# GNN kernel on one core: GpSimd makes histogram digits, ScalarE zeroes the sums, SyncE reads the rows of two steps at a time

## The reference

```python
# layer 0: attention over edges, two heads of 64
rel_t_enc = jnp.cos((last_update[src] - t)[:, None] * time_w + time_b)
edge_attr = jnp.concatenate([rel_t_enc, msg], axis=-1)
q, k, v = x @ Wq + bq, x @ Wk + bk, x @ Wv + bv
e = edge_attr @ We
alpha = sum(q[dst] * (k[src] + e)) / 8        # per head
a = segment_softmax(alpha, dst)
out = segment_sum((v[src] + e) * a, dst) + x @ Wskip + bskip
x = layernorm(x + out)
# layer 1: the same edges the other way round: gathered at dst, summed at src
agg = segment_sum(edge_weight[:, None] * x[dst], src)
x = layernorm(x + agg @ W.T + b)
```

## Time and profile before

| | |
|---|---|
| median of 3 runs | 9757.03 us (9748.06 to 9765.64) |
| the profiled execution | 9753.79 us, its span 9752.1 us |
| busy: DVE, PE, POOL, ACT | 88%, 78%, 68%, 52% |
| setup | 0 to 342 us |
| layer 0 and its norm | 342 to 5240 us |
| layer 1, with pairs | 5240 to 9347 us |
| the last steps of segments | 9347 to 9653 us |

### The profile page before, as it was taken

One profiled execution on the slowest core, in us unless ns is written; L12 is line 12 of the kernel. 1 busy time (PEld: TensorE's weight loads), 2 busy tenths in 40 slices (PEclk: granted clock), 3 DMA queues, 4 the chain that ended last, 5 costly groups with the idle time before them and its releaser, 6 DMA issues. The chain is left out here.

```text
span 9752.1 us, 272152 instructions
## 1 busy us (share of the span) xinstructions
PE 7647.0 (78%) x52868; PEld 7179.5 (74%) x52869; DVE 8623.8 (88%) x21301; ACT 5102.7 (52%) x20838; POOL 6585.4 (68%) x6871
## 2 busy tenths in 40 slices
PE   6477777777777777777765777888888888888865
PEld 2477777777777777777765777788888888888854
DVE  5899999999999999999988666799999999999968
ACT  2277777777777777777762333333333333333300
POOL 0477777777777777777754777777777777777720
PEclk8689889888988888888885555587888887878888
DMA  6477767667666777766652222355555555556554
GB/s 193 109 180 179 177 177 180 177 176 180 178 178 177 179 177 178 179 179 177 178 126 64 74 74 74 99 152 150 152 152 152 152 152 150 153 150 153 152 138 116
DMA packets 1631706, 1484.67 MB, mean 152 GB/s; under 512 B 792007, under 2 KB 1363043, under 8 KB 1631203
## 3 DMA queue, kind: packets, MB, share of 16 engines
q1 hardware_dynamic: 1374244, 848.34, 35.8%
q0 software_dynamic: 257088, 632.95, 23.1%
HBM read 1225.51 MB, written 254.87 MB: 152 GB/s over the span
## 5 line engine op out<-in xcount | busy, mean ns | idle before, releaser
L817 POOL DMA_INDIRECT kv<-kv_scratch,arena x3136 | 3250.7, 1037 | 1238.1 <-issue 839.8
L869 POOL DMA_INDIRECT message_scratch<-ohT,idx x3232 | 3100.3, 959 | 1086.1 <-issue 956.5
L1261 ACT ACTIVATE ohT<-bank,kv 128x128 f32<-128x128 f32 x3232 | 923.9, 369 | 2609.2 <-PE bank L1063 1866.5
L1154 ACT ACTIVATE arena<-arena,weights 128x65 f32<-128x65 f32 x7040 | 1771.7, 337 | 2.4 <-PE bank L982 2.3
L1077 PE MATMUL bank<-oh,kve 128*128 128x128 f32 x8640 | 1377.4, 319 | 140.9 <-DVE arena L1838 107.9
L1063 PE MATMUL bank<-acc,oh 128*128 x6464 | 1284.9, 361 | 214.4 <-ACT ohT L1262 213.6
L982 PE MATMUL bank<-arena,oh 128*128 128x130 f32 x7040 | 1162.1, 317 | 288.0 <-DVE acc L1670 282.3
L1077 PEld LDWEIGHTS bank<-oh,kve 128*128 128x128 f32 x8640 | 1230.3, 224 | 163.8 <-issue 151.7
L1063 PEld LDWEIGHTS bank<-acc,oh 128*128 128x128 f32 x6464 | 1142.8, 265 | 259.1 <-issue 258.3
L982 PEld LDWEIGHTS bank<-arena,oh 128*128 128x128 f32 x7040 | 1045.5, 226 | 369.9 <-issue 300.3
L973 PE MATMUL bank<-arena,ohT 128*128 128x128 f32 x7040 | 1093.4, 307 | 0.0
(11 more groups left out here) (232 smaller groups left out, 12885.1 us busy)
## 6 DMA issues: line engine op xcount, KB each, us to landing
kve<-message_scratch SPq DMA_DIRECT2D x2160, 129.0 KB
kve<-nodes_scratch SPq DMA_DIRECT2D x880, 256.0 KB
feat<-in_edge_attr_dram SPq DMA_DIRECT2D x880, 96.0 KB
feat<-block_scratch SPq DMA_DIRECT2D x812, 98.0 KB
arena<-q_scratch SPq DMA_DIRECT2D x880, 64.0 KB
message_scratch<-ohT,idx POOLq DMA_INDIRECT x3232
kv<-kv_scratch,arena POOLq DMA_INDIRECT x3136
feat<-in_edge_attr_dram SPq DMA_DIRECT2D x880, 32.0 KB
```

The lines of the kernel that those rows point to most:

```text
L817: pool.indirect_dma_start(kv[:, k, g, :], None, kv_d, bass.IndirectOffsetOnAxis(ap=group_rows[:, half, k * G + g, 0:1].bitcast(I32), axis= ...
L869: pool.indirect_dma_start(msg_d, bass.IndirectOffsetOnAxis(ap=idx[:, k, g:g + 1], axis=0), sum_ring[:, k % RING1, g, :], None).then_inc(s_ ...
L1154: op = act.activation(wv[:, st.k % 2, g, h, :], vR[:, st.k, g, h, :], ACT.Copy, scale=weights[:, st.k // ROUND, g, st.k % ROUND, h:h + 1])
L1261: act.activation(sum_ring[:, st.k % RING1, g, 0:C], banks[2 + st.k % 2][:, g * P:(g + 1) * P], ACT.Copy, scale=taken[:, st.k, g, 2:3])
```

## The change

1. POOL makes the digits `h_lo` and `h_hi` at the start, from the moment that DVE is done with `raw` (`s_hist` 3), with a scratch `h_ten` for the product that one fused DVE operation did before. It also writes the high one-hots, seven comparisons of 128x128 a chunk in place of one DVE operation. DVE keeps the low one-hots, PE waits for both.
2. ACT zeroes `acc` by a copy of a broadcast zero, after the last reader of the histogram (`s_hist` 25). DVE's memset is gone; its first addition to `acc` waits for ACT.
3. In the last steps (`pairs` False) SP reads the six row numbers of two steps at once, and DVE makes the differences between the first and the second addition instead of after the third.

```diff
+            def whole(out, at):
+                pool.wait_ge(s_hist, at)
+                pool.tensor_scalar(out, out, MAGIC, None, ALU.add).then_inc(s_hist, 1)
+                pool.wait_ge(s_hist, at + 1)
+                pool.tensor_scalar(out, out, MAGIC, None, ALU.subtract).then_inc(s_hist, 1)
+
+            pool.wait_ge(s_hist, 3)
+            pool.wait_ge(s_tw, NT + 1)
+            pool.wait_ge(s_const, 3)
+            pool.tensor_scalar(h_lo, srcf_t[:, 0:THIST], 1.0 / P, -(P - 1) / (2.0 * P), ALU.mult, ALU.add).then_inc(s_hist, 1)
+            whole(h_lo, 4)
+            pool.wait_ge(s_zero, 16 * (4 + -(-NT // PIECE)))
+            pool.wait_ge(s_hist, 6)
+            pool.tensor_scalar(h_hi, h_lo, 1.0 / 16, -7.5 / 16, ALU.mult, ALU.add).then_inc(s_hist, 1)
+            whole(h_hi, 7)
+            pool.wait_ge(s_hist, 9)
+            pool.tensor_scalar(h_ten, h_hi, -16.0, None, ALU.mult).then_inc(s_hten, 1)
+            pool.wait_ge(s_hten, 1)
+            pool.tensor_tensor(h_lo, h_lo, h_ten, ALU.add).then_inc(s_hist, 1)
+            pool.wait_ge(s_ndump, 16 * NDUMPS)
+            for j in range(H_CHUNKS):
+                n = min(P, THIST - j * P)
+                wait(pool, s_hmm, j - 1)
...
+                for b in range(7):
+                    op = pool.tensor_scalar(h_oh[j % 2][1][:, 0:n, b], h_hi[:, j * P:j * P + n], float(b), None, ALU.is_equal)
+                op.then_inc(s_hohi, 1)
...
                     pe.wait_ge(s_hoh, j + 1)
+                    pe.wait_ge(s_hohi, j + 1)
...
+            act.wait_ge(s_tab, 2)
+            act.wait_ge(s_hist, 25)
+            act.activation(acc[:, :], zero[:, 0:1].to_broadcast([P, NB * HEADS * HB]), ACT.Copy).then_inc(s_acc0, 1)
...
-            dve.tensor_scalar(h_lo, srcf_t[:, 0:THIST], 1.0 / P, -(P - 1) / (2.0 * P), ALU.mult, ALU.add).then_inc(s_hist, 1)
-            halves(h_lo, P, 4)
...
-                dve.tensor_tensor(h_oh[j % 2][1][:, 0:n, :], h_hi[:, j * P:j * P + n].unsqueeze(2).to_broadcast([P, n, 7]),
-                                  irow[:, 0:7].unsqueeze(1).to_broadcast([P, n, 7]), ALU.is_equal).then_inc(s_hoh, 1)
...
-            dve.memset(acc[:, :], 0.0)
...
+                if isinstance(st.s, int) and st.s == 0:
+                    dve.wait_ge(s_acc0, 1)
...
-                rows = several(mybir.EngineType.SP, seg_row_i[0:1, bass.ds(q, SEGMENT)], TRASH // 2 - P)
+                if k % at_once == 0:
+                    found = several(mybir.EngineType.SP, seg_row_i[0:1, bass.ds(q, SEGMENT * at_once)], TRASH // 2 - P)
...
+                    if segs and not pairs:
+                        seg(i, k, 0, 3, pairs, seg_rels)
                     if segs:
                         seg(i, k, 1, 0, pairs, seg_add)
...
-                    if segs:
+                    if segs and pairs:
                         seg(i, k, 0, 3, pairs, seg_rels)
```

More of the change, by code:

```diff
@@ L267, in build @@
         THIST = -(-TILES // 8) * 8
-        h_lo, h_hi = raw[:, 0, 0:THIST], raw[:, 2, 0:THIST]
+        h_lo, h_hi, h_ten = raw[:, 0, 0:THIST], raw[:, 2, 0:THIST], raw[:, 1, 0:THIST]
         h_oh = [[raw[:, 1, 1472 * k + a:1472 * k + b].bitcast(BF16).rearrange("p (t n) -> p t n", t=P) for a, b in ((0, 1024), (1024, 1472))] for k in range(2)]
@@ L333, in build @@
         s_hist, s_hoh, s_hmm = sem("s_hist"), sem("s_hoh"), sem("s_hmm")
+        s_hohi, s_hten, s_acc0 = sem("s_hohi"), sem("s_hten"), sem("s_acc0")
         H_CHUNKS = -(-THIST // P)
@@ L720, in row_load, with seg_loads @@
                              .to_broadcast([NB, G * P])).then_inc(s_msg[st.k], 16)
-            def seg_loads(i, k):
+            seg_rows = {}
+            def seg_loads(i, k, at_once=1):
                 q = PER * (i - BEGIN) + SEGMENT * k
-                rows = several(mybir.EngineType.SP, seg_row_i[0:1, bass.ds(q, SEGMENT)], TRASH // 2 - P)
+                if k % at_once == 0:
+                    found = several(mybir.EngineType.SP, seg_row_i[0:1, bass.ds(q, SEGMENT * at_once)], TRASH // 2 - P)
+                    for n in range(at_once):
+                        seg_rows[k + n] = found[SEGMENT * n:SEGMENT * (n + 1)]
+                rows = seg_rows[k]
                 first = Segment(Step1(i, k), 0)
@@ L745, in loads1 @@
                     if segs:
-                        seg_loads(i, k)
+                        seg_loads(i, k, 1 if pairs else 2)
             ROWS_AHEAD = 12
@@ L794, in _ @@
             pool.iota(istep_i[:, :], pattern=[[1, STEPS]], base=0, channel_multiplier=0).then_inc(s_iota, 1)
+            def whole(out, at):
[20 more added lines that the diff above has]
+                wait(pool, s_hmm, j - 1)
+                if j == 0:
+                    pool.wait_ge(s_hist, 10)
+                for b in range(7):
+                    op = pool.tensor_scalar(h_oh[j % 2][1][:, 0:n, b], h_hi[:, j * P:j * P + n], float(b), None, ALU.is_equal)
+                op.then_inc(s_hohi, 1)
             for k in range(2):
@@ L1418, in halves @@
                 dve.tensor_scalar(out, out, MAGIC, None, ALU.subtract).then_inc(s_hist, 1)
-            dve.wait_ge(s_zero, 16 * (4 + -(-NT // PIECE)))
-            dve.tensor_scalar(h_lo, srcf_t[:, 0:THIST], 1.0 / P, -(P - 1) / (2.0 * P), ALU.mult, ALU.add).then_inc(s_hist, 1)
-            halves(h_lo, P, 4)
[L1423 to L1427, removed]
+            dve.wait_ge(s_hist, 10)
             dve.wait_ge(s_ndump, 16 * NDUMPS)
-            dve.wait_ge(s_hist, 10)
             for j in range(H_CHUNKS):
@@ L1433, in _ @@
                 dve.tensor_tensor(h_oh[j % 2][0][:, 0:n, :], h_lo[:, j * P:j * P + n].unsqueeze(2).to_broadcast([P, n, 16]),
-                                  irow[:, 0:16].unsqueeze(1).to_broadcast([P, n, 16]), ALU.is_equal)
-                dve.tensor_tensor(h_oh[j % 2][1][:, 0:n, :], h_hi[:, j * P:j * P + n].unsqueeze(2).to_broadcast([P, n, 7]),
-                                  irow[:, 0:7].unsqueeze(1).to_broadcast([P, n, 7]), ALU.is_equal).then_inc(s_hoh, 1)
+                                  irow[:, 0:16].unsqueeze(1).to_broadcast([P, n, 16]), ALU.is_equal).then_inc(s_hoh, 1)
             by_bin = ident[:, :].rearrange("p (t l) -> p t l", l=16)
@@ L1481, in _ @@
             dve.wait_ge(s_hist, 24)
-            dve.tensor_scalar(at_seg[:, :], at_seg[:, :], float(P), None, ALU.mult)
+            dve.tensor_scalar(at_seg[:, :], at_seg[:, :], float(P), None, ALU.mult).then_inc(s_hist, 1)
             dve.wait_ge(s_tdump, 16)
```

## The result

The changed kernel takes 9854.47 us (median of 5 runs, 9847.2 to 9868.67), the kernel before beside it 9748.06; the ratio is 1.0106, with a 95% interval of 1.0094 to 1.0117. It is about 1.1% slower. The forecast was 9770 with a range that ended at 9812, and it gave "no difference that can be told" the same chance as "slower", 0.35: the time lies above the range. The profiled execution has a span of 9867.0 us, so its own time is the longest of the five; it is 114.9 longer than the profile before, where the medians differ by 106.

A forecast was written before the change was run, and what follows sets the result against it. SP was taken to bound the last steps, and one chain of nodes, histogram and tables the setup. Setup +27 −15.6 +25 −2 = +34, last steps −21, sum +13: 9770 us, range 9718 to 9812.

The forecast's parts named there:

- rival 3: Setup: POOL slow at 2.6 ns a column, nodes +41, histogram +46 −2, in all +48, 9805 us; chance 0.22.
- Digits off DVE: Setup, before the histogram: DVE no longer makes the digits, which shortens the chain by 15.6 us.
- Digits on POOL, price: Setup: a POOL digit operation over 3,128 columns costs 5.4 us, 1.75 ns a column, between 2.8 and 8.1.
- Nodes: Setup: POOL's operations hold up DVE's small ones, so the nodes start at about 109, not 82.4: +27 us.
- One-hots: Histogram: POOL's seven comparisons exclude DVE's low one-hot, 4.3 us a chunk: +25, and −2 for the first two chunks.
- ACT's zeroing: End of setup: ACT's copy replaces DVE's memset and hides in ACT's idle 18 us: 0.
- Tail: Last 120 steps: a load of six at 1.06 us makes SP's step 2.27 instead of 2.45: −21 us.
- Rival 4: Last steps: a load of six costs 1.34 or differences hold up additions, −5 instead of −21, 9786 us; chance 0.10.

The follow-up runs named there:

- setup-only: The changed kernel with the last steps of the kernel before (digits and high one-hots on POOL, zeroing on ACT): 9865.8 us, ratio 1.0117.
- highs-on-dve: The changed kernel with the high one-hots back on DVE, digits still on POOL: 9759.66 us, ratio 1.0004.
- tail-only: The kernel before with only the third part of the change (load of six, differences between additions): 9737.7 us, ratio 0.9984.
- four-at-once: Changed kernel, high one-hots on DVE, POOL digits as multiply-and-add, last five after the tables' piece, one twelve-value SP load per four last steps: ratio 0.9977.
- late-only: Changed kernel, high one-hots on DVE, POOL's last five digit operations waiting for the tables' piece, their arithmetic as in the change: ratio 0.9994.
- load-only: The kernel before with one SP load of six row numbers per two last steps, differences where they were: ratio 0.9998.
- The best kernel: Changed kernel, high one-hots on DVE, POOL digits as multiply-and-add, last five after the tables' piece; measured twice: ratios 0.9980 and 0.9977.

## Why the prediction was wrong

The mechanism of the loss was seen, and rival 3 had its sign; its size was not. By the steps of the sum:

- **Digits off DVE, −15.6**: right.
- **Digits on POOL, price**: taken at 5.4 each, between bounds of 2.8 and 8.1. The mean of the seven is 7.3, and none of them takes it: 2.80 and 5.72 for the two that multiply and add, 8.1 to 9.6 for the five with a single addition, subtraction or multiplication, so the upper bound was even passed. The row of the lower bound was a cast, that of the upper one, L855, in the kernel's code a single multiplication, the form of five of the seven; I averaged the two. Its 2.6 ns a column would have come close for these five.
- **Nodes, +27**: +37.3, by the mechanism described (one DVE operation to each of POOL's, `brow` last), inside the bound of +41. Then the nodes took 2 more in this trace (in setup-only 3 less: scatter).
- **One-hots, +25 −2**: +91 between the first and last low one-hot (73.7 before, 160.1 between the corresponding full chunks, and 7.7 to the short one in place of 3.2). This step failed: the term was sized at a quarter of what it is. The structure was right (POOL and the low one-hot exclude each other: 2.92 for the comparison that meets it), the price was not: 0.30 an operation forecast and 0.53 as the bound, where 0.92 was measured, four in seven of them 0.98 apart. I scaled a rate from operations that write whole rows of four-byte numbers; the new ones write two bytes in every fourteen. The bound of 0.53 left out the layout of the output. By highs-on-dve this one term is 95 to 100 us.
- **Last chunk**: put at nothing, for it is not in the sum. PE needs the last high one-hots too, POOL is behind by most of a chunk, and from the last low one-hot to the first table load it is 25.2 where it was 18.1.
- **ACT's zeroing, 0**: right, 10.82 and hidden.
- **Tail, −21**: −15.3 in the profiles, −16 in tail-only. The load of six at 1.06 came out near the mean of about 1.0, and that was luck: half of them take 0.72 and half 1.27. The prediction took the price to go by the number of values, on one load each of ACT and DVE; the row of eight values, under four-at-once, stood in the trace before and spoke against it. What the sum left out are the stalls between good steps: the mean pitch is 2.39 (284.4 over 119) where I had 2.27 for every step, and was 2.52 (299.7 over 119) where I had 2.45. Rival 4's differences that wait for a DMA exist, 8.3 us in 102 steps.
- **The rules of the Trainium skill.** "GPSIMD Engine Reference", section 4.1, calls one-input work roughly line-rate: the 0.89 ns a column of L817's mult and add agrees, the single addition's 2.6 ns and the strided comparison do not. The Trainium skill's "DMA: Bandwidth & Descriptors", section "Latency and other measured facts", puts a floor of some 600 ns under a register load, by which a load of six is hardly dearer than one of three: the quick half, 0.72 beside 0.67, and the twelve of four-at-once at 0.75 agree, the slow half at 1.27 does not.

The range failed for the same reason: its top, 9812, lies just above rival 3's 9805, which had 0.43 an operation. With 0.92 and the same structure, seven make 6.4 and the low one-hot 2.3, a period of 8.7 as an upper estimate; the measured 7.67 is a little below since some comparisons start 0.58 apart and overlap.

## What to carry over

An operation that moves to POOL is to be priced by its arithmetic, its element size and the stride of its output, and what it blocks on DVE is priced by counting DVE's operations beside it, not by their length; where no row shows the form, a hundred and more of them are a reason for a much wider range. Look up in the code which arithmetic a row stands for before taking its price. Here the pair mult and add cost a third of a single add over the same 3,128 columns, and 0.30 beside 0.53 over 128. Where two engines are within some per cent of each other in a loop, as SP and DVE here, expect little of speeding up either alone: it gave 4 us and 1, and both together 15 to 19. A median can be a time that nothing takes; look at the single ones when minimum and maximum lie far apart.

## What was not expected of the hardware

POOL's TENSOR_SCALAR over 3,128 columns: 2.80 us for mult and add, 8.12 to 8.36 for add or subtract, 9.60 for a multiplication by −16 (8.13 in late-only), 10.76 to 11.00 for add or subtract followed by an addition of 0. A register load of twelve values took 0.75 on SP, one of six 0.72 or 1.27. Two chips differed by a third for the same kernel, 9753.79 on one, 12979.35 and 12749.35 on the other, with setup and tail equal to some us. The mean granted TensorE clock was 0.81 on the first and 0.72 on the second, but in the tail 0.98 on both; whether the lower clock is a cause of the longer stages or goes with them is not shown. On the second chip ACT waited in layer 0 283 times, 1,454 us in all, for a releaser that the profile does not know, as in this row of load-only. The cause stays open.

```profile
3000.64 0.59 ACT L1167 ACTIVATE featT<-bank 96x512 f32<-96x512 f32 x1 [6.44 <-remote]
```

The best kernel, 26 us under the kernel before, was measured only on the second chip; on the first its gain is expected from the equal setup and tail, and not shown.
